# Attention scores kept as running sums of key differences in PSUM, with 64-row products in the two halves of the array

## The reference

```
q_hk = (hidden_q @ Wq.T).reshape(Bv, Sv, H, K)          # H = 16 heads
q_big = jnp.einsum('bshk,hkq->bshq', q_hk, w_kc_q)
q_big = _apply_rope(q_big, sin_q[None, :, None, :], cos_q[None, :, None, :])
kv_r = _apply_rope(kv_c, sin_k[None], cos_k[None])      # 1444 keys of 64, shared by all heads
q_r = jnp.einsum('bshq,hqr->bhsr', q_big, W_qr)
k_r = jnp.einsum('bld,hdr->bhlr', kv_r, W_kr)
scores = jnp.einsum('bhsr,bhlr->bhsl', q_r, k_r)
attn = jax.nn.softmax(scores, axis=-1)
ctx_c = jnp.einsum('bhsl,bld->bhsd', attn, kv_r)
ctx_lat = jnp.einsum('bhsd,hkd->bhsk', ctx_c, w_kc_kv)
```

## Time and profile before

| what | value |
|---|---|
| median of 3 runs | 3590.11 us (3571.32 to 3590.87) |
| the profiled execution | 3590.73 us, span 3588.9 us |
| granted TensorE clock, mean | 0.925 |
| PE busy | 3053.0 us (85%) |
| DVE busy | 2329.4 us (65%) |
| POOL busy | 1556.9 us (43%) |
| ACT busy | 1339.3 us (37%) |
| score products (L1423, L1424) | 576.3 and 536.4 us busy, 1536 each |
| maxima (L1340) | 328.7 us busy, 1344 products |
| reductions of maxima (L1139) | 745.3 us busy, 448 |

### The profile page before, as it was taken

One profiled execution on the slowest core, in us unless ns is written; L12 is line 12 of the kernel. 1 busy time (PEld: TensorE's weight loads), 2 busy tenths in 40 slices (PEclk: granted clock), 3 DMA queues, 4 the chain that ended last, 5 costly groups with the idle time before them and its releaser, 6 DMA issues. The chain is left out here.

```text
span 3588.9 us, 55868 instructions
## 1 busy us (share of the span) xinstructions
PE 3053.0 (85%) x16648; PEld 2035.5 (57%) x16656; DVE 2329.4 (65%) x3226; ACT 1339.3 (37%) x2810; POOL 1556.9 (43%) x1035
## 2 busy tenths in 40 slices
PE   6999879998699989989989998998998999897244
PEld 4777679997455545555555564555555556454123
DVE  5777754454766666666666666666666666664887
ACT  1322322222144344424424434443443443443356
POOL 0000022221554545544645554554554555553566
PEclk9988889999899999989999999999999999998566
DMA  3000010002100000000000000000000000000100
GB/s 103 0 0 0 0 49 9 5 9 51 28 19 17 17 13 20 16 10 20 21 8 20 16 17 13 21 15 15 15 21 9 21 15 17 8 14 26 67 12 24
DMA packets 129556, 70.00 MB, mean 20 GB/s; under 512 B 83566, under 2 KB 123854, under 8 KB 129224
## 3 DMA queue, kind: packets, MB, share of 16 engines
q1 hardware_dynamic: 129288, 66.79, 7.4%
HBM read 56.30 MB, written 10.04 MB: 18 GB/s over the span
## 5 line engine op out<-in xcount | busy, mean ns | idle before, releaser
L1080 POOL TENSOR_TENSOR c_psum<-c_p 120x800 f32<-120x800 f32 (+1 forms) x384 | 749.1, 1956 | 807.1 <-ACT c_p L1298 513.1
L1139 DVE TENSOR_REDUCE c_mneg<-c_m_ps 128x1 fp32r<-128x1452 f32 (+1 forms) x448 | 745.3, 1664 | 407.5 <-PE c_m_ps L1340 406.8
L1298 ACT ACTIVATE c_p<-c_s_ps 120x400 f32<-120x400 f32 (+1 forms) x1536 | 655.0, 509 | 774.9 <-PE c_s_ps L1424 772.8
L1437 PE MATMUL c_o_ps<-c_p,c_val 120*64 120x400 f32 (+1 forms) x3072 | 598.8, 511 | 0.0
L1423 PE MATMUL c_s_ps<-c_q,c_k 128*120 128x400 f32 (+1 forms) x1536 | 576.3, 375 | 10.1 <-ACT c_q L1246 8.8
L1424 PE MATMUL c_s_ps<-c_q,c_k 128*120 128x400 f32 (+1 forms) x1536 | 536.4, 349 | 0.0
L1340 PE MATMUL c_m_ps<-c_k,c_q 64*128 64x484 f32 (+1 forms) x1344 | 328.7, 445 | 131.8 <-DVE c_mneg L1139 104.7
L1073 POOL TENSOR_TENSOR c_rot<-c_psum,c_rs 96x400 f32<-96x400 f32 x256 | 259.9, 1038 | 308.5 <-DVE c_rs L1181 304.9
L1423 PEld LDWEIGHTS c_s_ps<-c_q,c_k 128*120 128x120 f32 (+1 forms) x1536 | 283.3, 184 | 178.5 <-issue 161.7
L1437 PEld LDWEIGHTS c_o_ps<-c_p,c_val 120*64 120x64 f32 (+1 forms) x3072 | 187.0, 136 | 275.0 <-issue 143.1
L1340 PEld LDWEIGHTS c_m_ps<-c_k,c_q 64*128 64x128 f32 (+1 forms) x1344 | 130.7, 175 | 347.0 <-DVE c_mneg L1139 233.4
(11 more groups left out here) (220 smaller groups left out, 4161.4 us busy)
## 6 DMA issues: line engine op xcount, KB each, us to landing
c_rdb<-l_denominators SPq DMA_DIRECT2D x128, 100.0 KB, 2.7
c_kv<-in_ctx SPq DMA_DIRECT2D x32, 360.0 KB
c_q<-c_mneg SPq DMA_DIRECT2D x384, 0.5 KB, 1.9
c_den<-c_oden SPq DMA_DIRECT2D x256, 0.8 KB
x_rows<-in_x SPq DMA_DIRECT2D x4, 800.0 KB
x_spill<-x_rows SPq DMA_DIRECT2D x8, 400.0 KB
c_xa<-x_spill SPq DMA_DIRECT2D x8, 400.0 KB
c_xr<-x_spill SPq DMA_DIRECT2D x32, 100.0 KB
```

The costliest lines, as they stand in the source:

```text
L1080: g.tensor_tensor(psum[0:k, u % 2, :], p[0:k, 2 * u % 4, :], p[0:k, (2 * u + 1) % 4, :], ALU.add).then_inc(psum_ready, 1)
L1139: v.tensor_reduce(mneg[0:n, c, t:t + 1], m_ps[0:n, :, 0:4 * KP], AX.XY, ALU.max, negate=True).then_inc(mneg_ready, 1)
L1298: a.activation(p[0:k, w % 4, i * HALFQ:(i + 1) * HALFQ], s_ps[0:k, (2 * w + i) % 4, 0:HALFQ], ACT.Exp).then_inc(exp_ready, 1)
L1437: mm = pe.matmul(o_ps[i * DL:(i + 1) * DL, 0:HALFQ], val[0:k, j % 2, r, :], p[0:k, w % 4, i * HALFQ:(i + 1) * HALFQ], start=(r == 0), stop ...
```

## The change

Scores are made as running sums. The sum in a score bank is not started anew for each tile: tile r adds to what tile r - 2 left in the same bank, after ACT has read it, and what is added is queries times (keys of tile r minus keys of tile r - 2). Only tiles 0 and 1 of a chunk start a bank, with a **seed**: a product of a matrix with one row of ones (`first`) and the row of maxima (`mrow`). A product then needs no row for the maxima, and each 64-row product is put in one half of the array: the low half takes the first 400 queries, the high half the other 400. A tile is six products of 64 rows: high keys by high queries, low keys by high queries, high keys by low queries, each in both halves.

The differences are formed by POOL (`difference`, five steps of two tiles, from the last tiles to the first), from keys that ACT copies out of PSUM in full precision (`kd`). After that ACT rounds the differences, into both halves of c_k1 (six operations), DVE subtracts (three, now at pair 8) and ACT copies the low part to the upper half (three). The maxima use rounded keys of their own (`kmax`), copied from PSUM at once. Where ACT's nine steps stand is given by tables, HEAD_STEPS and TILE_STEPS. The seventh maxima block takes the last 128 queries instead of 32, with 64 rows.

```
--- before.py
+++ after.py
+        HEAD_STEPS = {10: (0, 1), 11: (2,), 12: (3,), 13: (4, 5), 14: (6, 7), 15: (8,)}
+        TILE_STEPS = {14: (0,), 15: (1,), 16: (2,), 17: (3, 4), 18: (5,), 19: (6,), 20: (7,), 21: (8,)}
...
+                def difference(b, r):
+                    if r == NT - 2:
+                        g.wait_ge(kf_ready, PRIMED + (b + 1) * 3)
+                    else:
+                        g.wait_ge(kd_ready, PRIMED + b * 5 + (NT - 2 - r) // 2)
+                    g.sem_inc(m.carrier, 1)
+                    new, old = slice(r * KP, (r + 2) * KP), slice((r - 2) * KP, r * KP)
+                    g.tensor_tensor(kd[:, new], kd[:, new], kd[:, old], ALU.subtract).then_inc(kd_ready, 1)
...
+                        if j + 1 < G and at in (5, 6):
+                            for r in ((10, 8, 6), (4, 2))[at - 5]:
+                                difference(b + 1, r)
...
-                for i in range(2):
-                    g.memset(k2[i][0:DL, :].bitcast(F32), 1.0).then_inc(consts, 1)
...
-                g.memset(q2[0:DL].bitcast(F32), 0.0).then_inc(consts, 1)
+                g.memset(mrow[:].bitcast(F32), 0.0).then_inc(consts, 1)
...
+                def round_keys(b):
+                    v.wait_ge(kf_ready, PRIMED + b * 3 + 1)
+                    v.tensor_copy(klow[:, 0:4 * KP], m_ps[0:DL, 0, 0:4 * KP]).then_inc(kmax_low, 1)
+                    v.wait_ge(kf_ready, PRIMED + b * 3 + 3)
+                    v.tensor_copy(klow[:, 8 * KP:12 * KP], m_ps[0:DL, 2, 0:4 * KP]).then_inc(kmax_low, 1)
...
+                        v.tensor_tensor(k2[j % 2][0:DL, cols], kd[:, cols], k1[j % 2][0:DL, cols].bitcast(F32),
                                         ALU.subtract).then_inc(k1_ready, 1)
...
+                        if j + 1 < G and (c, q) == (1, 2):
+                            split_keys(it * G + j + 1, j + 1)
...
+                def round_steps(b, j, n):
+                    cols = slice(n % 3 * 4 * KP, (n % 3 + 1) * 4 * KP)
+                    if n < 6:
+                        a.wait_ge(kd_ready, PRIMED + (b + 1) * 5)
+                        a.sem_inc(m.carrier, 1)
+                        a.activation(k1[j % 2][n // 3 * DL:(n // 3 + 1) * DL, cols], kd[:, cols], ACT.Copy).then_inc(k1_hi, 1)
+                    else:
+                        a.wait_ge(k1_ready, PRIMED + b * 3 + n - 5)
+                        a.sem_inc(m.carrier, 1)
+                        a.activation(k2[j % 2][DL:128, cols], k2[j % 2][0:DL, cols].bitcast(F32), ACT.Copy).then_inc(k2_ready, 1)
...
-                            if w % CT in (10, 11, 12) and j + 1 < G:
-                                place_keys(it * G + j + 1, j + 1, w % CT - 10)
+                            for n in TILE_STEPS.get(w % CT, ()) if j + 1 < G else ():
+                                round_steps(it * G + j + 1, j + 1, n)
...
+                    pe.matmul(m_ps[:, 0, 0:4 * KP], q1[low, j, q], klow[:, 0:4 * KP], start=True, stop=True)
+                    pe.matmul(m_ps[:, 1, 0:4 * KP], q1[high, j, q], khigh[:, 4 * KP:8 * KP], start=True, stop=True)
+                    mm = pe.matmul(m_ps[:, 2, 0:4 * KP], q1[low, j, q], klow[:, 8 * KP:12 * KP], start=True, stop=True)
...
+                        if w >= 2:
+                            pe.wait_ge(exp_ready, PRIMED + 2 * it * NU + 2 * w - 2)
...
-                            pe.matmul(o, k1[j % 2][:, r * KP:r * KP + k], q1[:, j, cols], start=True, stop=False)
-                            mm = pe.matmul(o, k2[j % 2][:, r * KP:r * KP + k], q2[:, j, cols], start=False, stop=True)
-                            mm.then_inc(s_ready, 1)
+                        if r < 2:
+                            for i in range(2):
+                                pe.matmul(bank[i][0:KP], first[side[i], :], mrow[side[i], c, :], start=True, stop=False, skip_group_check=True)
+                        for i in range(2):
+                            pe.matmul(bank[i][0:k], k1[j % 2][side[i], keys], q1[side[i], j, q[i]], start=False, stop=False, skip_group_check=True)
+                        for i in range(2):
+                            pe.matmul(bank[i][0:k], k2[j % 2][side[i], keys], q1[side[i], j, q[i]], start=False, stop=False, skip_group_check=True)
+                        for i in range(2):
+                            pe.matmul(bank[i][0:k], k1[j % 2][side[i], keys], q2[side[i], j, c, :], start=False, stop=True, skip_group_check=True).then_inc(s_ready, 1)
```

114 lines of the change are left out of this document (66 added, 48 removed).

## The result

The changed kernel takes **3663.92 us** (median of 4 runs, 3650.98 to 3667.15) against 3582.93 us for the kernel before in the same session (4 runs): ratio **1.022, 95% interval 1.018 to 1.027**. It is 81 us slower, where 18 were forecast, and lies outside the range. The profiled execution took 3667.15 us, span 3665.3 us, mean clock 0.909 (before 0.925).

The account below looks back on a forecast made before the run. It took PE as the bound only in part, many score products hiding behind DVE's reductions. Groups +2.2 us times eight (+17), start -4, clock +5 gave 3608 us from 3590.1; range 3545 to 3655.

Parts of the forecast that it names:

- The split on DVE: Subtractions at pair 8, between reciprocal and slot 18's reduction: 1.1 us later per later batch, 0.55 in the first.
- the gain at the start: At the start of the stage, POOL's smaller memset holds back DVE's four operations less: 4 us less, once.
- S before slot 12: A pair's score products (S) shorten and slot 12's maxima wait less: -1.96 us in the first batch, -1.62 later.
- Slot 15: Maxima in slot 15 wait for ACT's copy, behind roundings awaiting POOL's differences: 2.3 us lost in 24 of 32 batches.
- The clock: Waits before slots 15 and 19 may lower TensorE's granted clock: 0.2 us on each of 24 batches, +5 us.
- rival 1: Lower clock stays through values and scores after slot 19: 1.7 us in each of 24 batches, 3644 us; chance 0.22.
- Rival 3: Half-array products do not overlap in a long series: a pair's scores take 2.3 us, 3800 us and more; chance 0.05.
- rival 2: Slot 15 waits little, its differences being shorter or earlier ready, with no clock cost: 3548 us; chance 0.17.
- Its own signs: Wrong if scores exceed 2 us, slot 15 starts within 7.5 us of slot 12, or group time changes over 6 us.
- the half products' gain: A pair's score products as 64-row halves take 1.28 us instead of 1.65; forecast's terms gave 61 us over the run.

Follow-up runs that it names:

- Experiment 5: Changed kernel with GpSimd's additions of pairs 7, 8 and 9 cut to 8 columns in a group's first three batches; 3608.78 us, ratio 1.009.
- Experiment 1: Changed kernel with all five key differences on GpSimd placed behind pair 5's addition; 3625.95 us, ratio 1.014.
- experiment 13: Changed kernel with 40 filling products on TensorE in the wait before slot 19's maxima; 3648.46 us, ratio 1.020.
- experiment 2: Changed kernel with VectorE's three subtractions cut to 8 columns in a group's second to fourth batch; 3608.26 us, ratio 1.008.
- experiment 4: Changed kernel with Experiment 1's edit, subtractions moved ahead of pair 7's jobs and ScalarE's roundings one pair earlier; 3594.93 us, ratio 1.005.
- experiment 6: Against experiment 4: third subtraction moved ahead of pair 8's jobs, context product behind the jobs of pairs 4 and 10; 3574.55 us, ratio 0.9996.

## Why the prediction was wrong

- **The split on DVE (the step that failed).** The term was "three splits took 1.79; POOL now adds at the same time, ... so I add 0.5 for that, and take back 0.7". The 0.5 came from one row, an addition of 1.70 us, that had met only the end of POOL's, as POOL's list of before shows:

```profile
1090.78 3.74 POOL L1080 TENSOR_TENSOR c_psum<-c_p 120x800 f32<-120x800 f32 x2 [5.34 <-ACT c_p L1298]
```

  POOL was done at 1094.52, and DVE's addition 0.85 us later. It was no operation of 0.98 us slowed by 0.7, but one that waited. The splits took 3.76 to 3.81 us in the first group (up to 4.09 in the run), 1.5 more than the 2.3 of the forecast. The 0.7 was given back (that addition now takes 0.97), but from the reciprocal to the next first S it took 13.52 us (1085.30 to 1098.82) where 11.5 were forecast: 1.5 from this and some 0.5 for the clock. Experiment 5 shows the cause: POOL short, DVE at 1.80 us. What was needed was in the trace of before: 135 of DVE's additions and context products there begin while a POOL operation runs, and end 0.85 and 0.43 us after it. So was the earlier trace rows, DVE's four normalisations, 10.23 us beside a 5.42 us memset; in the changed kernel these take 1.79 us. I used that row for the gain at the start (4 us; it alone gave 8.4) and not for the price at pair 8. The Trainium skill's page "SBUF — State Buffer", section "SBUF: two separate sides", says that VectorE and GpSimd share a pair of ports as an exclusive lock, and that a VectorE instruction with two inputs in SBUF contends with a GpSimd instruction that reads SBUF. This trace agrees: 2.32 us for an operation of 0.64, done 0.51 us after POOL's end.
- **S before slot 12.** -1.62 was forecast, -1.0 measured in later batches, -0.4 in the first. S itself is right (1.29 us), and so is the count of S that hide in a loop of two slots. Part of the saving is given back at slots 6 to 8. DVE adds sums between the reductions of slots 6 and 7, and that addition took 1.65 us beside POOL (1053.29) where it took 1.08 before (1061.56): slots 6 to 8 take 5.51 us instead of 5.05. It is the same pattern at a second place, read from the lists and not tested. In the first batch the clock is the larger part: it fell to 0.50 behind slot 8's wait of 1.47 us, and the values and the transposes there took 2.15 and 2.41 us instead of 1.56 and 1.40.
- **Slot 15** was right in its place and, at 1.9 to 2.3 for 2.3, in its size. Its releaser was as forecast (ACT's first rounding waits 2.52 us for POOL's c_kd). Experiment 1 prices it at 38 us (55 in the sum). A difference took 0.61 us; the line through the two rows gives 0.69 and not the 0.67 of the text, and the rate without a fixed part 0.53 and not 0.4, neither of which matters here.
- **The clock.** The forecast put 5 us for it and rival 1 put 41. The wait at slot 19 was 4.95 us instead of the "up to 2.8" counted (which left out the forecast's own 0.5 for the splits: with it, 3.3); experiment 13 prices the fall at 15 to 24 us. The clock fell behind slot 19's wait in all 24 batches. It fell behind slot 15's as well in 9 of them, and there, as the prediction had it, the slow products ended in time spent waiting: slots 15 to 18 took 0.7 us longer and slot 18 to 19 the same 7.03 us. But slot 19's wait did not shrink by it, and stayed at 4.92 to 4.96. Rival 1's place was right; its wait was 2.8 us long, and its price is some 1.0 a batch instead of 1.7.
- **Rival 3** (halves that don't overlap, S = 2.3 us) is out at 1.29 us; **rival 2** is not what happened, though experiment 1 shows what it would have been worth: 38 us, not 60.
- **Its own signs.** The prediction called itself wrong if group time changed by more than 6 us. It changed by 10.9.

The prices do not simply add: 38 (experiment 1), 55 (experiment 5, with what it takes from other operations) and 15 to 24 (experiment 13, part of which is in the 55) stand against 81 net of the gains. What remains open is the rest of the half products' gain: forecast 61, alone 17 to 30, with short reductions 27 to 29, and 45 for the whole change in the good order. That the waits at slots 12, 19 and 20 and at the first S take it is read from the lists, not tested.

## What to carry to other kernels

- Before a DVE operation is placed, look at what POOL does in the same microseconds. Price it as "until POOL's operation ends, plus its own time less 0.13 us", as in the rows here, not with a surcharge, and above all where another engine waits for what is queued behind it.
- A stretch with PE busy at 92% can still be set by a loop through another engine. Follow the M-reduction-M distance: where it does not change with PE's work, less PE work becomes a wait, and what pays is the order in that other engine's queue. Here a handful of moves in the queues of DVE, POOL and ACT turned a loss of 81 us into a gain of 67.
- When one operation in front of a waited-for reduction is removed, read the queue again for the next one before a gain is promised: experiments 2, 4 and 6 each fell short by that.

## What the runs showed of the hardware that I had not expected

- VectorE's operations on SBUF operands stand beside GpSimd's (0.64 to 2.32 us, 0.56 to 2.20 us, 0.98 to 2.70 us). The reduction out of PSUM keeps its 1.65 to 1.67 us in all 448 cases of the changed kernel's trace, 316 of which overlap an operation of GpSimd by over 0.3 us.
- It goes the other way too. Most of GpSimd's 384 additions of 800 columns took 1.87 to 1.94 us, but 48 took 2.0 to 2.7: those of them that I read began while an SBUF operation of VectorE ran. One that began at 1098.92, 0.16 us after an addition of VectorE's, took 2.59 us.
- 64-row products in array halves keep a start of 0.18 us per pair of halves over 12 products in a row, and need no gap behind a block of maxima in the same form (1008.77 to the first score product at 1009.10).
- Filling a wait of PE's with 128x112 products kept the granted clock up (1.00 in the stretch that 84 of them filled, and behind slot 19 in 17 of 24 batches with 40) and gained 15 us net by the medians; each cost 0.107 us.
